# Attention block and quantised MLP on one core: seven of the eight rows of reciprocal deviations made by two transfers through DRAM

## The chip, the core and the metric

The kernel runs on one core of a Trainium2 chip. The metric is the time of one launch on the device in microseconds (us), as the median of the runs shown. The shortened names are those of the profile: PE is TensorE, PEld its weight loads, DVE VectorE, ACT ScalarE, POOL GpSimd, SP SyncE; SPq is SP's queue of DMA issues.

## The reference, cut to what matters

```python
def reference(x, ctx, g_xattn, g_ffn, Wq, ...):
    # x: (2, 2048, 512); ctx: (2, 77, 512); 16 heads of 32
    q = proj(_layernorm(x), Wq, bq)          # (x - mean) / sqrt(var + 1e-5), per token
    k, v = proj(ctx, Wk, bk), proj(ctx, Wv, bv)
    attn = softmax(q @ k.T / sqrt(32)) @ v   # per head
    x = x + tanh(g_xattn[0]) * (attn @ Wo.T + bo)
    h = gelu(_qlinear(_layernorm(x), w1, b1))  # inputs and weights rounded to 8 bits per tensor
    x = x + tanh(g_ffn[0]) * _qlinear(h, w2, b2)
    return x                                  # all in float32
```

The part that matters here is the first layer norm. Its mean is taken out by centring `Wq`; its factor 1/sqrt(var + eps) differs from token to token and is multiplied onto the projected q.

## The kernel before

The 4096 tokens are worked through in `NC` = 8 chunks of `CH` = 512 tokens, each of `TT` = 4 tiles of 128 tokens. The program has three stages, each a block of its own: `attention` (until some 337 us), `hidden` (first matmul of the MLP) and `output` (second). Only `attention` is touched. In it five instruction streams are written out by hand, one per engine, and meet at semaphores; their order is the order of the calls in each engine's `first_step`, `step(i)` for i = 1 to 7 (`LAST` = 7) and `last_steps`. `AHEAD` = 2: chunk 2's q is projected partly in step 1.

q is computed transposed, with features on the partitions and tokens along the row. So the factor of a token has to lie along the row too, the same on all 128 partitions: that is the tile `row` (128x512). It is made per chunk n like this:

- DVE's `stats1(n)` (L980, L984) gives mean and variance with the tokens on the partitions; POOL's `rstd_1(n)` (L1248, L1252) makes `rstd1`, 128x4: element (p, t) belongs to token 128 t + p.
- PE's `row_turn(n)` (L413) makes four 128x128 transposes of the broadcast columns of `rstd1` into a bank of PSUM.
- ACT's `row_copy(n)` (L760) copies that bank into `row`. It waits until q of the chunk before is scaled, as there is one `row`.
- DVE's `q_scale(n, m)` (L999), m = 0 to 3, multiplies each of the four banks of projected q by `row`.

From there the chain inside a step runs over three engines, once for each of four feature blocks m: PE's `project_q(i, m)` (L475), DVE's `q_scale(i, m)` (L999), ACT's `q_high(i, m)` (L780), PE's `scores_by_token(i, m)` (L488), DVE's `token_max(i, m)` (L1017), with DVE's `q_low(i, m)` (L1003) in between. `scores_by_token(i, m + 1)` writes the banks that `token_max(i, m)` reads, and waits for it. After the fourth, PE's `transpose_max(i)` (L502) turns the maxima. PE fills the time with pieces of the output projection of chunk i-2 (`project_out`, L578), in step 1 with chunk 2's projection (`project_q_ahead`, L453). `row_turn(i + 1)` stands in step i right behind `scores_by_token(i, 2)`, `row_copy(i + 1)` on ACT behind `q_high(i, 3)`:

```python
project_q(i, 3)
scores_by_token(i, 2)
if i < LAST:
    row_turn(i + 1)
if older:                      # i >= 2
    pe.wait_ge(q_lo_on, KD * i + 3)
    project_out(i - 2, 2, 0, 7)
...
scores_by_token(i, 3)
```

The last step, i = 7, has the same order but no next chunk, so no `row_turn`. `row_turn(1)` stands in PE's `first_step`, between the sums of head group 1 and `scores_by_key(0, 3)`; behind that comes `values(0, 2)` (L534), which waits for ACT's `c_copy(0, 1)` (L804). On ACT `c_copy(0, 1)` stands behind `xt_high(1, 2)` and `xt_high(1, 3)` (L774), which read the tile `xr` that SP loads.

SP issues nearly all transfers, in one order. Around the change that is, at the end of chunk 0: `load_x(2)`, `load_xt(1, 2)`, `load_xt(1, 3)` (L347, 256 KB of transposed x each into one of two slots of `xr`, once POOL's `xt_low` has freed it), four `load_xt_ahead` (L351, 256 KB each), `load_x(3)` (L340, 1 MB). Then per step: four `load_xt` of the next chunk, `load_x` of a later one, `store_x1` of an older one. ACT issues transfers only at the start.

Of the kernel before, what the change touches and what calls it, by code (L numbers as in the profile page):

```python
# [14 lines left out]
F32 = mybir.dt.float32  # L15
# [7 lines left out]
P = 128  # L23
# [39 lines left out]
def program(nc, x, x_t, ctx_t, wq_t, wk_t, wv_t, wo_t, bq, bk, bv, bo, w1_t, b1, w2_t, b2, g_xattn, g_ffn,  # L63
            eye, group_ones, out):
    with ExitStack() as whole:
# [21 lines left out]
        sh.ps = whole.enter_context(nc.psum_tensor("ps", [P, 8, 512], F32))  # L87
        sh.x1_dram = nc.dram_tensor("x1_dram", [NC, P, TT, D], F32, kind="Internal").ap()
# [38 lines left out]
def attention(nc, sem, sh, x, x_t, ctx_t, wq_t, wk_t, wv_t, wo_t, bq, bk, bv, bo, w1_t, b1, g_xattn, g_ffn,  # L127
# [8 lines left out]
    with ExitStack() as own:  # L136
# [103 lines left out]
        row_on = sem("row_on")  # L240
        q_scaled = sem("q_scaled")
# [66 lines left out]
        def rstd_value(c):  # L308

            return c + 1  # L310
# [15 lines left out]
        with nc.Block() as block:  # L326
            @block.sync
            def _(sp):
# [19 lines left out]

                def load_xt_ahead(k):
                    sp.wait_ge(w_lo_on, KD)  # L350
                    sp.dma_start(wo_raw[:, k, :], xt_v[k, AHEAD]).then_inc(xt_ahead_in[k], 16)  # L351
# [29 lines left out]
                load_x(2)  # L381
                load_xt(1, 2)
                load_xt(1, 3)
                for k in range(KD):
                    load_xt_ahead(k)
                sp.wait_ge(v_on, B)
                load_x(3)
                for i in range(1, NC):
                    n = i + 1
                    if AHEAD < n < NC:  # L390
                        load_xt(n, 0)
                        load_xt(n, 1)
                        load_xt(n, 2)
                        load_xt(n, 3)
                    if W1_T // TT <= i + 2 < NC:
                        load_x(i + 2)
                    if i >= 2:
                        store_x1(i - 2)
# [5 lines left out]
            def _(pe):  # L404
                def row_turn(n):

                    pe.wait_ge(ln1_rstd, rstd_value(n))
                    if n >= 2:
                        pe.wait_ge(c_on, GROUPS * (n - 1))
                    elif n == 1:  # L410
                        pe.wait_ge(v_on, B)
                    for t in range(TT):
                        mm = nc.tensor.transpose(ps[:, row_bank(n), t * P:(t + 1) * P],  # L413
                                                 rstd1[:, t:t + 1].to_broadcast([P, P]), sh.ident[:])
                    mm.then_inc(row_mm, 1)
# [43 lines left out]
                def project_q(c, m):  # L459
                    if m >= 2:  # L460
                        pe.wait_ge(q_lo_on, KD * c + m - 1)
                        if c == AHEAD:
                            pe.wait_ge(x1_on, TT * (c - 2) + m - 1)
                    elif c >= 2:
                        pe.wait_ge(x1_on, TT * (c - 2) + m + 1)
                    elif m == 0:
                        pe.wait_ge(v_on, 1)
                    else:
                        pe.wait_ge(row_on, 2)
# [23 lines left out]
                def transpose_max(c):  # L493
                    pe.wait_ge(smax_on, KD * c + KD)
                    if c == 0:
                        pe.wait_ge(q_lo_on, KD)
                    elif c < LAST:
                        pe.wait_ge(row_on, c + 2)
                    else:
                        pe.wait_ge(c_on, GROUPS * c)  # L500
# [102 lines left out]
                def first_step():  # L603
# [28 lines left out]
                    for g in range(1, GROUPS):  # L632
                        scores_by_key(0, g)
                        values(0, g - 1)
                        sums(0, g - 1)
                        if g == 2:
                            row_turn(1)

                def step(i):
# [15 lines left out]
                    if i < LAST:  # L655
                        row_turn(i + 1)
# [79 lines left out]
            def _(act):  # L736
# [100 lines left out]
                def first_step():  # L837
# [31 lines left out]
                    row_copy(1)  # L869
                    c_copy(0, 2)  # L870

                def step(i):
# [16 lines left out]
                    if nxt:  # L889
                        row_copy(n)  # L890
# [70 lines left out]
            def _(dve):  # L961
# [33 lines left out]
                def q_scale(c, m):  # L995
                    dve.wait_ge(q_mm, KD * c + m + 1)
                    dve.wait_ge(row_on, c + 1)
# [247 lines left out]
            def _(pool):  # L1245
                def rstd_1(c):
# [3 lines left out]
                    if c:  # L1250
                        pool.wait_ge(row_mm, c)
# [722 lines left out]
```

## Time and profile before

| | |
|---|---|
| median of 3 runs | 580.91 us (580.72 to 581.07) |
| the profiled execution | 581.38 us, of it 579.6 us span |
| PE busy | 565.7 us (98%), 3272 matmuls |
| DVE, ACT, POOL busy | 442.1 (76%), 336.6 (58%), 300.8 us (52%) |
| granted TensorE clock | 0.999 |
| DMA | 106.62 MB, mean 184 GB/s |

Busy matmuls are modelled with their ends overlapping the next one's start: in attention a 128x512 matmul is shown with some 0.39 us but follows its neighbour after 0.23 us, so a PE that is busy all the time can still have short waits inside. They are better read from the starts. In the timeline a row is one instruction, or a run of equal ones (x4), with start, duration, engine, line, operation, output and inputs, and in brackets the engine's idle time before it with what ended it.

### The profile page before, as it was taken

What the parts mean: (1) busy time and instruction counts of PE and PEld (TensorE: products, weight loads), DVE (VectorE), ACT (ScalarE), POOL (GpSimd) and SP (SyncE); (2) the same over time, 40 slices, a digit from 0 to 9 for tenths busy, and PEclk for the clock granted to TensorE, in tenths of its full rate; (3) what the DMA queues carried; (4) which work ended last, traced back from release to release, by engine and by line L of the source; (5) the groups of instructions that cost most, each with busy time, mean ns of one, the idle gap of its engine ahead of it and who ended that gap; (6) DMA issues with size and microseconds to landing.
All of it is one profiled execution on the core that took longest, in us unless ns stands there. A gap on an engine that the chain in (4) does not pass through costs nothing. (4 is left out here: it accounts for less than half of the span.)

```text
span 579.6 us, 9118 instructions
## 1 busy us (share of the span) xinstructions
PE 565.7 (98%) x3272; PEld 321.6 (55%) x3272; DVE 442.1 (76%) x622; ACT 336.6 (58%) x408; POOL 300.8 (52%) x242
## 2 busy tenths in 40 slices
PE   6999999999999999999999989999999999999997
PEld 3834746567476575674765854444444544444443
DVE  4698986979878698695895778788887799835282
ACT  3355374763855737438247538777786696555350
POOL 5457565762763666716072429655507247503383
PEclk9999999999999999999999999999999999999999
DMA  8966000411503305111001169987778995979766
GB/s 310 384 280 219 1 2 0 155 65 31 185 4 110 110 0 183 37 37 75 0 1 74 72 217 336 368 325 278 284 278 327 368 320 217 340 297 390 228 235 218
DMA packets 41944, 106.62 MB, mean 184 GB/s; under 512 B 3377, under 2 KB 4145, under 8 KB 37297
## 3 DMA queue, kind: packets, MB, share of 16 engines
q1 hardware_dynamic: 39952, 103.70, 48.8%
q10 hardware_dynamic: 1952, 2.42, 1.2%
q8 instruction: 23, 0.38, 0.3%
q14 instruction: 17, 0.13, 0.1%
HBM read 64.16 MB, written 41.94 MB: 183 GB/s over the span
## 5 line engine op out<-in xcount | busy, mean ns | idle before, releaser
L1552 PE MATMUL ps<-h_sb,w_q 128*128 (+1 forms) x488 | 109.7, 379 | 0.1
L1851 PE MATMUL ps<-w_q,h_q 128*128 128x512 bf16 x448 | 96.9, 379 | 0.0
L1934 POOL TENSOR_TENSOR xo<-xo,b2s 128x512 f32<-128x512 f32 x32 | 52.5, 1672 | 70.4 <-DMA xo<-x_dram 52.4
L1552 PEld LDWEIGHTS ps<-h_sb,w_q 128*128 128x128 bf16 x488 | 46.7, 98 | 52.2 <-issue 1.1
L1851 PEld LDWEIGHTS ps<-w_q,h_q 128*128 128x128 bf16 x448 | 43.8, 98 | 52.9
L1619 ACT ACTIVATE xo<-ps,b1s,sc 128x1024 f32<-128x1024 f32 x48 | 57.6, 1205 | 20.0 <-PE ps L1552 16.7
L794 ACT ACTIVATE prob<-ps 77x1024 f32<-77x1024 f32 x64 | 61.7, 1013 | 10.6 <-PE ps L521 10.6
L1705 DVE TENSOR_REDUCE hmax<-xo 128x1024 f32 (+1 forms) x48 | 58.3, 1217 | 12.1 <-ACT xo L1619 11.4
L1738 POOL TENSOR_SCALAR y<-x,mean,rs 128x512 f32<-128x512 f32 x24 | 50.2, 2098 | 29.6 <-DVE xq L1686 23.2
L780 ACT ACTIVATE q_hi<-ps,bq_sb 128x512 fp32r<-128x512 f32 x32 | 22.0, 688 | 63.8 <-DVE ps L999 63.6
L1286 POOL TENSOR_TENSOR c_lo<-c_sb,c_hi 128x512 fp32r<-128x512 f32 x28 | 38.4, 1391 | 34.6 <-ACT c_hi L822 34.6
L1911 DVE SCALAR_TENSOR_TENSOR xo<-ps,hs,xo 128x512 f32<-128x512 f32 x32 | 23.3, 746 | 40.3 <-POOL xo L1934 39.8
L1256 POOL TENSOR_TENSOR xt_lo<-xr,xt_hi 128x512 fp32r<-128x512 f32 x24 | 30.6, 1296 | 34.7 <-ACT xt_hi L774 34.5
L1017 DVE TENSOR_REDUCE neg_max<-ps 128x16 f32<-128x1232 f32 x32 | 45.9, 1433 | 3.3 <-PE ps L488 3.3
L578 PE MATMUL ps<-wo_hi,c_hi 128*128 128x512 f32 x112 | 47.3, 422 | 0.0
L578 PE MATMUL ps<-wo_hi,c_lo 128*128 128x512 f32 x112 | 44.9, 401 | 0.0
L578 PE MATMUL ps<-wo_lo,c_hi 128*128 128x512 f32 x112 | 44.2, 395 | 0.0
L1883 ACT ACTIVATE h_q<-h_sb 128x2048 bf16<-128x2048 f32 x16 | 29.7, 1902 | 20.9 <-DVE h_sb L1904 11.0
L475 PE MATMUL ps<-xt_hi,wq_hi 128*128 128x512 f32 x104 | 41.7, 401 | 0.0
L475 PE MATMUL ps<-xt_hi,wq_lo 128*128 128x512 f32 x104 | 40.9, 393 | 0.0
L475 PE MATMUL ps<-xt_lo,wq_hi 128*128 128x512 f32 x104 | 40.7, 391 | 0.0
L1301 POOL TENSOR_TENSOR x<-x,bo_gate 128x512 f32<-128x512 f32 x32 | 40.3, 1293 | 0.1
(194 smaller groups left out, 1110.5 us busy)
## 6 DMA issues: line engine op xcount, KB each, us to landing
h_dram<-xo SPq DMA_DIRECT2D x48, 512.0 KB, 2.9
h_sb<-h_dram SPq DMA_DIRECT2D x16, 1024.0 KB, 11.2
x_dram<-x SPq DMA_DIRECT2D x8, 1024.0 KB, 3.9
xo<-x_dram SPq DMA_DIRECT2D x8, 1024.0 KB, 5.0
x<-h_dram SPq DMA_DIRECT2D x8, 1024.0 KB, 7.8
x<-in_x SPq DMA_DIRECT2D x7, 1024.0 KB, 7.1
out<-xo SPq DMA_DIRECT2D x7, 1024.0 KB, 8.5
xr<-in_x_t SPq DMA_DIRECT2D x24, 256.0 KB, 3.7
```

Source lines behind the costliest of these rows:

```text
L475: mm = nc.tensor.matmul(ps[:, q_bank(c, m), :], w[:, k, m * P:(m + 1) * P], r[:, k, :], start=(j == 0), stop=(j == len(terms) - 1))
L578: mm = nc.tensor.matmul(ps[:, bank, :], a[:, k, t * P:(t + 1) * P], w[:, k, :], start=(j == 0), stop=(j == len(terms) - 1))
L794: nc.scalar.activation(prob[0:NK, p % SLOTS, :].rearrange("p (s n) -> p s n", s=2), ps[0:NK, 2 * (p % 2):2 * (p % 2) + 2, :], ACT.Exp).the ...
L1017: nc.vector.tensor_reduce(neg_max[:, :, :].rearrange("p t (r j) -> p t r j", j=DK)[:, :, :, m], ps[:, 0:TT, 0:4 * NK].rearrange("p t (h n) ...
L1286: nc.gpsimd.tensor_tensor(lo[:, g, :], c_sb[:, g, :], hi[:, g, :].bitcast(F32), ALU.subtract).then_inc(c_lo_on, 1)
L1301: nc.gpsimd.tensor_tensor(xa, xa, sh.bo_gate[:], ALU.add).then_inc(xg_on, 1)
L1552: mm = nc.tensor.matmul(ps[:, 2 * (m % 2) + s, :], w1_q[:, k, m * P:(m + 1) * P], xq_t[:, one(2 * j + s), k, :], start=(k == 0), stop=(k = ...
L1619: nc.scalar.activation(dst.rearrange("p (s n) -> p s n", s=2), ps[:, bank:bank + 2, :], ACT.Gelu, bias=b1s[:, m:m + 1], scale=sc[:, 4:5]). ...
L1705: nc.vector.tensor_reduce(dst, src, AX.X, ALU.max, apply_absolute_value=True).then_inc(hmax_on, 1)
L1738: nc.gpsimd.tensor_scalar(y[:, n % YS, :], x1[:, n, :], sh.mean2[:, n:n + 1], rs2[:, n:n + 1], ALU.subtract, ALU.mult).then_inc(y_on, 1)
L1851: mm = nc.tensor.matmul(ps[:, 4 * s + t, :], h_q[s][:, m, t * P:(t + 1) * P], w2_q[:, m, :], start=(m == 0), stop=(m == MF - 1))
L1934: nc.gpsimd.tensor_tensor(xo[:, s, t, :], xo[:, s, t, :], b2s[:], ALU.add).then_inc(xb_on, 1)
```

## The change

For chunks 1 to 7 PE's `row_turn` and ACT's `row_copy` go. Their place is taken by two transfers that SP issues: `store_row(n)` writes `rstd1` (128x4) to a row of 512 words in DRAM, so that element (p, t) lands at word 128 t + p, and `load_row(n)` reads that row back, broadcast to 128 partitions (256 KB), into `row`. `load_row(n)` waits for the store's end, for `q_scaled` of the chunk before (as `row_copy` did) and for the row load before. Chunk 0 keeps the old way.

```diff
+        sh.row_dram = nc.dram_tensor("row_dram", [NC, CH], F32, kind="Internal").ap()
...
+                def store_row(n):
+                    sp.wait_ge(ln1_rstd, rstd_value(n))
+                    sp.dma_start(sh.row_dram[n].rearrange("(t p) -> p t", p=P), rstd1[:],
+                                 allow_slow_non_contiguous=True).then_inc(row_out, 16)
+
+                def load_row(n):
+                    sp.wait_ge(row_out, 16 * n)
+                    sp.wait_ge(q_scaled, scaled_count(n - 1, KD - 1))
+                    if n >= 2:
+                        sp.wait_ge(row_in, 16 * (n - 1))
+                    sp.dma_start(row[:], as_row(sh.row_dram[n]).to_broadcast([P, CH])).then_inc(row_in, 16)
...
                 sp.wait_ge(k_biased, GROUPS)
                 load_x(2)
+                store_row(1)
                 load_xt(1, 2)
                 load_xt(1, 3)
+                load_row(1)
                 for k in range(KD):
                     load_xt_ahead(k)
...
                 for i in range(1, NC):
                     n = i + 1
+                    if n < NC:
+                        store_row(n)
                     if AHEAD < n < NC:
                         load_xt(n, 0)
                         load_xt(n, 1)
+                    if n < NC:
+                        load_row(n)
+                    if AHEAD < n < NC:
                         load_xt(n, 2)
                         load_xt(n, 3)
...
     # row_turn
                     pe.wait_ge(ln1_rstd, rstd_value(n))
-                    if n >= 2:
-                        pe.wait_ge(c_on, GROUPS * (n - 1))
-                    elif n == 1:
-                        pe.wait_ge(v_on, B)
...
     # project_q(1, 1)
-                        pe.wait_ge(row_on, 2)
+                        pe.wait_ge(v_on, B)
...
     # transpose_max
-                    elif c < LAST:
-                        pe.wait_ge(row_on, c + 2)
                     else:
                         pe.wait_ge(c_on, GROUPS * c)
...
     # PE, first_step and step
-                        if g == 2:
-                            row_turn(1)
...
-                    if i < LAST:
-                        row_turn(i + 1)
...
     # ACT, first_step and step
-                    row_copy(1)
...
-                        row_copy(n)
...
     # q_scale
-                    dve.wait_ge(row_on, c + 1)
+                    if c:
+                        dve.wait_ge(row_in, 16 * c)
+                    else:
+                        dve.wait_ge(row_on, 1)
...
     # rstd_1
-                    if c:
-                        pool.wait_ge(row_mm, c)
+                    if c == 1:
+                        pool.wait_ge(row_mm, 1)
+                    elif c:
+                        pool.wait_ge(row_out, 16 * (c - 1))
```

How this moves the instructions stands below at the two places that the prediction speaks of. On PE, in step 2 around the turn for chunk 3 (`k_hi,q_hi` are the scores by token, `wo` pieces of the output projection, `neg_max` the turned maxima), before:

```order
L488 MATMUL ps<-k_hi,q_hi 128x308 [waits smax_on,q_hi_on]
L488 MATMUL ps<-k_hi,q_hi 128x308 x3
L413 MATMUL ps<-ident,rstd 128x128 [waits c_on,ln1_rstd]
L413 MATMUL ps<-ident,rstd 128x128 x3
L578 MATMUL ps<-wo_hi,c_hi 128x512 [waits q_lo_on]
...
L578 MATMUL ps<-wo_hi,c_hi 128x512
L488 MATMUL ps<-k_hi,q_hi 128x308 [waits smax_on,q_hi_on]
L488 MATMUL ps<-k_hi,q_hi 128x308 x3
...
L502 MATMUL ps<-ident,neg_max 128x128 [waits row_on,smax_on]
```

and now:

```order
L506 MATMUL ps<-k_hi,q_hi 128x308 [waits smax_on,q_hi_on]
L506 MATMUL ps<-k_hi,q_hi 128x308 x3
L594 MATMUL ps<-wo_hi,c_hi 128x512 [waits q_lo_on]
...
L594 MATMUL ps<-wo_hi,c_hi 128x512
L506 MATMUL ps<-k_hi,q_hi 128x308 [waits smax_on,q_hi_on]
L506 MATMUL ps<-k_hi,q_hi 128x308 x3
...
L518 MATMUL ps<-ident,neg_max 128x128 [waits c_on,smax_on]
```

The four transposes are gone from between the two score groups, and `transpose_max` waits for `c_on` in place of `row_on`. The same goes for steps 3 to 6.

On SP, from the load of x of chunk 2 on, before:

```order
L340 DMA x<-in_x 128x4x512 [waits x_in,k_biased]
L347 DMA xr<-in_x_t 128x512 [waits xt_lo_on] x2
L351 DMA w_i<-in_x_t 128x512 [waits w_lo_on] x4
L340 DMA x<-in_x 128x4x512 [waits x_in,v_on]
L347 DMA xr<-in_x_t 128x512 [waits xt_lo_on] x4
L340 DMA x<-in_x 128x4x512 [waits w1_narrow,x_in]
L357 DMA x_dram<-x 128x2048 [waits x1_on]
```

and now, in which `row_dram<-rstd` is `store_row` and `row<-row_dram` is `load_row`:

```order
L343 DMA x<-in_x 128x4x512 [waits x_in,k_biased]
L354 DMA row_dram<-rstd 128x4x1 [waits ln1_rstd]
L350 DMA xr<-in_x_t 128x512 [waits xt_lo_on] x2
L362 DMA row<-row_dram 128x512 [waits q_scaled,row_out]
L366 DMA w_i<-in_x_t 128x512 [waits w_lo_on] x4
L343 DMA x<-in_x 128x4x512 [waits x_in,v_on]
L354 DMA row_dram<-rstd 128x4x1 [waits ln1_rstd]
L362 DMA row<-row_dram 128x512 [waits row_in,q_scaled,row_out]
L354 DMA row_dram<-rstd 128x4x1 [waits ln1_rstd]
L350 DMA xr<-in_x_t 128x512 [waits xt_lo_on] x2
L362 DMA row<-row_dram 128x512 [waits row_in,q_scaled,row_out]
L350 DMA xr<-in_x_t 128x512 [waits xt_lo_on] x2
```

The store of row 1 now stands ahead of `xr` for (1, 2) and (1, 3), and the load of row 1 between them and the four loads ahead. From chunk 3 on all loads of `xr` stand behind the store of their chunk's row, and the last two also behind the load of the row.

## Rows read from the trace of the kernel before

**Rows 1.** Busy times by stretch: PE, PEld, DVE, ACT, POOL; last clock, DMA share, GB/s.

```profile
60.00:100.00 40.00, 39.84 (x258) 25.29 (x257) 32.11 (x52) 22.27 (x31) 21.92 (x20) 1.00 0.00 1
100.00:300.00 200.00, 199.97 (x1293) 128.24 (x1295) 163.27 (x249) 112.08 (x162) 110.33 (x103) 1.00 0.21 72
```

**Rows 2.** The copy's instructions (L760) in the whole run, ns min/median/max.

```profile
L760 ACT COPY row<-ps x8: 578/579/587, 23.3 to 254.1; 128x512 f32<-128x512 f32 x8
```

**Rows 3.** Timeline of step 6, around the turn for chunk 7.

```profile
253.09 0.60 PE L413 MATMUL ps<-ident,rstd 128*128 128x128 f32 x4
253.34 1.43 DVE L1017 TENSOR_REDUCE neg_max<-ps 128x16 f32<-128x1232 f32 x1
...
253.45 0.48 PE L578 MATMUL ps<-wo_hi,c_hi 128*128 128x512 f32 x1
...
255.17 0.72 PE L488 MATMUL ps<-k_hi,q_hi 128*128 128x308 f32 x4
...
255.92 1.44 DVE L1017 TENSOR_REDUCE neg_max<-ps 128x16 f32<-128x1232 f32 x1 [0.50 <-PE ps L488]
...
257.42 0.20 PEld L502 LDWEIGHTS ps<-ident,neg_max 128*128 128x128 f32 x2 [0.34 <-DVE neg_max L1017]
```

**Rows 4.** Timeline of step 7, the same place without a turn.

```profile
291.64 1.43 DVE L1017 TENSOR_REDUCE neg_max<-ps 128x16 f32<-128x1232 f32 x1
...
293.19 0.58 PEld L488 LDWEIGHTS ps<-k_hi,q_hi 128*128 128x128 f32 x4 [0.44 <-issue]
...
294.07 1.44 DVE L1017 TENSOR_REDUCE neg_max<-ps 128x16 f32<-128x1232 f32 x1 [0.34 <-PE ps L488]
...
295.56 0.20 PEld L502 LDWEIGHTS ps<-ident,neg_max 128*128 128x128 f32 x2 [0.35 <-DVE neg_max L1017]
```

**Rows 5.** Timeline of DVE, step 1, to chunk 2's first scaling.

```profile
66.00 0.70 DVE L999 TENSOR_TENSOR ps<-ps,row 128x512 f32<-128x512 f32 x1 [0.63 <-PE ps L475]
66.61 1.43 DVE L1017 TENSOR_REDUCE neg_max<-ps 128x16 f32<-128x1232 f32 x1
...
69.02 1.44 DVE L1017 TENSOR_REDUCE neg_max<-ps 128x16 f32<-128x1232 f32 x1 [0.32 <-PE ps L488]
70.42 0.70 DVE L999 TENSOR_TENSOR ps<-ps,row 128x512 f32<-128x512 f32 x1
...
74.89 0.75 DVE L1003 SCALAR_TENSOR_TENSOR q_lo<-ps,bq_sb,q_hi 128x512 fp32r<-128x512 f32 x1 [0.74 <-ACT q_hi L780]
```

**Rows 6.** Timeline of DVE, step 2, third and fourth maxima.

```profile
100.30 1.43 DVE L1017 TENSOR_REDUCE neg_max<-ps 128x16 f32<-128x1232 f32 x1
...
102.74 1.44 DVE L1017 TENSOR_REDUCE neg_max<-ps 128x16 f32<-128x1232 f32 x1 [0.35 <-PE ps L488]
```

**Rows 7.** Timeline at the end of chunk 0, SP and POOL and ACT and PE.

```profile
40.38 1.26 POOL L1252 TENSOR_TENSOR rstd<-ve,minus_half 128x4 f32<-128x4 f32 x1
...
42.78 1.57 SPq L347 DMA_DIRECT2D xr<-in_x_t  x2
...
44.40 1.85 SPq L351 DMA_DIRECT2D w_i<-in_x_t  x4
...
46.89 0.65 PE L413 MATMUL ps<-ident,rstd 128*128 128x128 f32 x4
46.96 0.61 ACT L774 CAST xt_hi<-xr 128x512 fp32r<-128x512 f32 x1
...
48.37 0.62 ACT L774 CAST xt_hi<-xr 128x512 fp32r<-128x512 f32 x1 [0.80 <-DMA xr<-in_x_t]
...
49.62 1.06 PE L534 MATMUL ps<-prob,v 128*32 128x512 f32 x8 [0.99 <-ACT c_sb L804]
```

**Rows 8.** Landing of the 24 loads of xr (L347), us from issue.

```profile
DMA to landing us min/median/max: 2.8/3.7/11.3
```

**Rows 9.** DMA packets between 18.2 and 18.6 us.

```profile
DMA packets 205, 0.09 MB, mean 218 GB/s; under 512 B 132, under 2 KB 173, under 8 KB 205
```

**Rows 10.** DMA queue of SP between 41.5 and 48.5 us.

```profile
q1 hardware_dynamic: 621, 1.14, 57.7%
```

More of the change, by code:

```diff
@@ L240, in attention @@
         row_on = sem("row_on")
+        row_out = sem("row_out")
+        row_in = sem("row_in")
         q_scaled = sem("q_scaled")
```

## The prediction

> **What bounds the kernel now.** I read the busy times by stretch first: over 200 us of attention PE is busy for 199.97 us [rows 1]. Read by itself, this says that whatever leaves PE is won whole. But the ends of matmuls are modelled, and short waits hide in them, so the second look goes to the timeline at the place of the change. In step 6 the turn starts at 253.09 and the next matmul at 253.45, so it holds PE for 0.36 us; the fourth maximum on DVE (L1017) starts at 255.92, and `transpose_max` (L502) at 257.42, released by DVE [rows 3]. DVE's third maximum starts at 253.34. Step 7 has the same order without a turn, and so shows what is left when the turn goes: there PE's weight loads stand still for 0.44 us ahead of the fourth score (L488), the fourth maximum starts 294.07 - 291.64 = 2.43 us behind the third, and L502 again waits for DVE, for 0.35 us [rows 4]. With the turn the same distance is 255.92 - 253.34 = 2.58 us [rows 3]. So this place is bound by the chain score, maximum, score, maximum over PE and DVE, and the turn lies mostly in a wait that is there anyway. The rest of a step is PE's, so what this place gives reaches the end.
>
> **The change part by part.** Seven of the eight turns go, four matmuls each [rows 3], and seven of the eight copies of 579 ns on ACT [rows 2].
>
> *Steps 3 to 6 (turns for chunks 4 to 7).* From the third maximum to L502 it is 257.42 - 253.34 = 4.08 us with a turn [rows 3] and 295.56 - 291.64 = 3.92 us without [rows 4]. That is 0.16 us a step, 0.64 us for four. The bound above is the 0.36 us that PE is held, 1.44 us for the four; I take the lower since step 7 is the very same code. Nothing is lost on DVE or ACT, which only move with it.
>
> *Step 2 (chunk 3).* The two maxima are 102.74 - 100.30 = 2.44 us apart [rows 6], already step 7's 2.43 us, as DVE is late here: the turn was hidden. Gain 0, at most 0.36.
>
> *Step 1 (chunk 2).* 69.02 - 66.61 = 2.41 us [rows 5]: gain 0, at most 0.36. Here alone the new path is short of time. The load of row 2 has to wait for the last scaling of chunk 1, which starts at 66.00 and takes 0.70 [rows 5], and the first scaling of chunk 2 wants the row at 70.42 [rows 5]: 3.7 us. The load has the size and the shape of a load of `xr`, whose landing takes 2.8 us at the least and 3.7 in the median [rows 8]. So it comes just in time. What DVE can bear beyond that is at least the 0.74 us that it idles later ahead of `q_low(2, 0)` [rows 5]. Cost 0; its cover is that slack, and without it the wait passes into the divisions and on to the output projection of chunk 0. The other six rows are asked for as early and wanted only in the next step.
>
> *The copies on ACT.* In steps ACT waits behind them for L502 anyhow; `xt_high` comes 0.5 us sooner, and nobody waits for it. 0.
>
> *Waits moved.* POOL's next factors now wait for the store of the row before, a step old by then: 0. SP now waits for POOL's factors ahead of loads of `xr`; for chunk 3 two of them move from the end of chunk 0 behind step 1, for the others they move by the last `xt_low` and the factors, two or three instructions of POOL, at the end of a step. All are wanted by `xt_high` only after the fourth projection of the next step: 0. `project_q(1, 1)` and `transpose_max` wait for something earlier than before: 0.
>
> *The end of chunk 0 (turn for chunk 1).* PE's turn at 46.89 wins nothing by itself, as PE then waits 0.99 us for ACT's `c_copy(0, 1)` until 49.62, and ACT had waited 0.80 us, until 48.37, for the second load of `xr` [rows 7]. So here a transfer sets the time. Both loads are issued within 42.78 to 44.35, and the four loads ahead come right behind them from 44.40 [rows 7]: the late one needed some 4.3 us. The change alters its company. Behind it, SP now stops for the end of the store of row 1 and then issues the load of that row, so the four loads ahead come later. In front of it stands the store: POOL has the factors at some 41.4 (its instruction starts at 40.38 and the next at 41.36) [rows 7], and SP sends 512 separate words, since neighbouring words of a partition lie 128 apart in DRAM. How long these take is the one price that the trace does not have. Bound from below: at 18.2 to 18.6 us the queues moved 205 packets in 0.4 us, 132 of them under 512 B [rows 9]; at that pace 512 are through in 1.0 us, before the first load of `xr` gets going. Bound from above by packets of 2 KB: 57.7% of 16 engines for 7 us is 64.6 us for 621 packets, 104 ns each [rows 10], so 512 on 16 engines hold them for 3.3 us. With 1 us from an issue to its first packet (my estimate, inside the shortest landing of 2.8 us [rows 8]) the store begins at 42.4 and is done at 43.4 or at 45.7, and the first load of `xr`, issued at 42.78, would begin at 43.8 without it. In the first case the second load of `xr` lands in the median 3.7 us [rows 8] after some 44.0, at 47.7, and ACT wants it at 46.96 + 0.61 = 47.57 [rows 7]: the 0.80 us are won nearly whole. In the second it lands up to 1.9 us later than that, 1.2 us after the old 48.37: a loss. The value lies nearer to the small packets' pace, because these are small packets, but reads are not writes; I take half of the gain, 0.4 us.
>
> The Trainium skill has a rule against just this edit: "DMA: Bandwidth & Descriptors", section "Rules for kernel authors", says that a strided last dimension becomes one descriptor per element and should be rearranged; section "Specifications" adds that under 512 B an engine reads, changes and writes back. No row here shows such a write. By it the store would be the third rival below, not the sum.
>
> **Sum** against the profiled execution, 581.38 us: 0.64 + 0.4 = 1.0, so 580.4 us. It stands 0.47 above the median of the three runs; against that median, 580.91 - 1.0 = **579.9 us**. 0.2% is 1.16 us, about what a measurement of this kernel can tell from no change; the forecast lies just within it.
>
> **The rivals.**
>
> *The transfer gap closes whole, and more of the turns comes back.* 0.64 + 0.80 = 1.44 us: 579.5. For it: the late load loses its company of four, and the words may be through before it begins. Against it: the unknown write. With 0.3 from step 1 or 2 it is 579.2. Chance 0.31.
>
> *PE is bound as its 99.98% says.* Every turn returns its 0.36 us [rows 3]: 7 x 0.36 = 2.5 us, 578.4. For it: PE's busy time [rows 1]. Against it: step 7 [rows 4], and the wait of 0.99 us behind the first turn [rows 7]. Chance 0.09.
>
> *The store blocks the loads of `xr` (slower).* Each word costs the engines a read and a write of the price of a whole packet, 2 x 104 ns [rows 10]: 512 of them hold 16 engines 6.7 us, from 42.4 to 49.1. If the same queue serves its transfers in order, the first load of `xr` then starts 5.3 us later than 43.8, and the second lands near 53.0, 4.6 us after the old one. ACT and PE wait that long once: 4.6 - 0.64 = 4.0 us more, 584.9. It decides from about 120 ns a word, where the loss passes 1.8 us. The other six stores stand where `xr` is wanted only much later. The rule of the Trainium skill on transfers under 512 B (same page, "Specifications") is this case. Chance 0.09.
>
> *Row 2 lands late (slower).* If the load of row 2 takes as long as the longest of `xr`, 11.3 us [rows 8], it lands 7.6 us after it is wanted; less the slack of 0.74 this is up to 6.9 us, less 1.0 of gain: 586.8. It decides when landing passes some 6 us (3.7 to the need, 0.74 of slack, 1.8 to leave the 0.2%). Against it: between 60 and 100 us the DMA engines are idle (share 0.00) [rows 1], so nothing is in its way. Chance 0.04.
>
> That the change does not do what it says is no rival: in the order of the changed program the turns and copies are gone.
>
> **How the numbers follow.** Forecast 0.47, within 0.2%. Faster: 0.31 + 0.09 = 0.40. Slower: 0.09 + 0.04 = 0.13. The range leaves out most of the full return of the turns and most of the slow cases, and takes in a small loss at the first loads (up to 1.2 us at 104 ns a word, and some beyond): 578.8 to 582.0.
>
> **What would show it.** In steps 3 to 6 the third and fourth maximum should stand 2.43 us apart in place of 2.58, with a wait ahead of the fourth score like that of step 7. Steps 1 and 2 should keep 2.41 and 2.44. At the end of chunk 0 PE's wait ahead of L534 tells the rest: if what it waits for comes at 48.8, the whole gap was won; if after 49.6, the store was in the way. The first scaling of chunk 2 should start with a wait under 0.8 us. The forecast is wrong if the median lies under 579.2 (more of the turns was PE's than step 7 shows) or above 581 (a transfer is waited for).

## The result and the profile after

The changed kernel takes 592.0 us (median of 4 runs, 590.9 to 592.9) against 580.99 us of the kernel before beside it: a ratio of 1.0186, 95% interval 1.0171 to 1.0201, or 11.0 us more. 579.9 us were forecast, in a range of 578.8 to 582.0. The profiled execution took 592.02 us, 590.2 us of it span, where the one before had 579.6.

The page shows little of it: PE is busy for 566.7 us in place of 565.7. What differs are the small packets.

```profile
span 590.2 us, 9062 instructions
...
PE 566.7 (96%) x3244; PEld 319.2 (54%) x3244; DVE 441.9 (75%) x622; ACT 333.4 (56%) x401; POOL 300.9 (51%) x242
...
DMA packets 46647, 108.47 MB, mean 184 GB/s; under 512 B 7184, under 2 KB 7952, under 8 KB 42000
```

3377 packets under 512 B before, 7184 now: of the 3807 more, 7 x 512 = 3584 are the words of the seven stores.

**Where the time went: one mark per step.** The transposes of the maxima (L502 before, L518 now) come once a step, so their starts date the loss. Before they start at 36.82, 70.52, 104.23, 142.53, 180.82, 219.12, 257.42 and 295.56 us; now (six of the eight) at:

```profile
36.63 0.42 PEld L518 LDWEIGHTS ps<-ident,neg_max 128*128 128x128 f32 x4 [1.55 <-DVE neg_max L1030]
...
80.27 0.42 PEld L518 LDWEIGHTS ps<-ident,neg_max 128*128 128x128 f32 x4 [0.55 <-DVE neg_max L1030]
...
115.13 0.42 PEld L518 LDWEIGHTS ps<-ident,neg_max 128*128 128x128 f32 x4 [0.34 <-DVE neg_max L1030]
...
153.25 0.42 PEld L518 LDWEIGHTS ps<-ident,neg_max 128*128 128x128 f32 x4 [0.34 <-DVE neg_max L1030]
...
267.60 0.42 PEld L518 LDWEIGHTS ps<-ident,neg_max 128*128 128x128 f32 x4 [0.34 <-DVE neg_max L1030]
...
305.71 0.42 PEld L518 LDWEIGHTS ps<-ident,neg_max 128*128 128x128 f32 x4 [0.34 <-DVE neg_max L1030]
```

From mark to mark: from the first to the second 43.64 in place of 33.70 us (+9.94; the end of chunk 0 and step 1), then 34.86 in place of 33.71 (+1.15), four times 38.12 on average in place of 38.30 (-0.18 each), then 38.11 in place of 38.14. These add up to +10.3; -0.2 at the first mark and some +0.5 behind attention make up the 10.6 us by which the span grew. So almost all of the loss is one event early on, and the gain of steps 3 to 6 is there. From the last mark to the end all kernels of this document run the same code, and yet their profiled executions take between 283.7 and 285.6 us for it. Differences of 1 us between whole times are therefore better read from the marks.

**The event.** Timeline of the changed kernel, SP's DMA issues with the row:

```profile
41.49 0.38 SPq L354 DMA_DIRECT2D row_dram<-rstd  x1
42.60 1.58 SPq L350 DMA_DIRECT2D xr<-in_x_t  x2
50.84 0.33 SPq L362 DMA_DIRECT2D row<-row_dram  x1
69.36 0.38 SPq L354 DMA_DIRECT2D row_dram<-rstd  x1
77.39 0.34 SPq L362 DMA_DIRECT2D row<-row_dram  x1
```

The load of row 1 waits for its store and is issued 9.35 us behind it; that of row 2, with no other transfer in the way, 8.03 us behind its own. ACT, PE and DVE, in the same stretch:

```profile
54.82 1.26 ACT L786 CAST xt_hi<-xr 128x512 fp32r<-128x512 f32 x2 [7.94 <-DMA xr<-in_x_t]
...
56.71 1.94 PE L550 MATMUL ps<-prob,v 128*32 128x512 f32 x8 [8.62 <-ACT c_sb L816]
...
64.17 1.06 PE L550 MATMUL ps<-prob,v 128*32 128x512 f32 x8
...
82.71 0.70 DVE L1012 TENSOR_TENSOR ps<-ps,row 128x512 f32<-128x512 f32 x1 [2.50 <-DMA row<-row_dram]
```

ACT waits 7.94 us for the second pair of `xr`, where it waited 0.80 [rows 7], and PE stands behind ACT's copy until 56.71 in place of 49.62: 7.1 us. The same eight matmuls of PE that start there take 1.94 us in place of 1.06, and the next such group starts at 64.17 in place of 54.44 (9.7 us later). So 2.6 us more go between those two. The granted clock says why:

```profile
50.00:55.00 5.00, 0.00 (x0) 0.00 (x0) 2.99 (x3) 0.18 (x1) 0.00 (x0) 0.71 0.64 118
55.00:60.00 5.00, 3.29 (x16) 0.68 (x16) 0.00 (x0) 3.95 (x6) 4.48 (x4) 0.50 0.97 340
60.00:65.00 5.00, 5.00 (x24) 3.17 (x24) 0.70 (x1) 0.00 (x0) 5.00 (x5) 0.77 0.16 60
```

Columns as in [rows 1]: PE did nothing from 50 to 55 us, and from 55 to 60 us the clock granted is 0.50, which is 1.2 of 2.4 GHz; before, these windows show 1.00. The 0.71 from 50 to 55 us shows that the clock fell while PE was still waiting; the price of 2.6 us is paid after the wait. Last, row 2 comes 2.50 us late for chunk 2's first scaling.

**What the DMA engines did.** The same two stretches in the DMA view, of the changed kernel:

```profile
DMA packets 528, 0.00 MB, mean 2 GB/s; under 512 B 528, under 2 KB 528, under 8 KB 528
```

```profile
DMA packets 97, 0.19 MB, mean 28 GB/s; under 512 B 9, under 2 KB 9, under 8 KB 96
...
q1 hardware_dynamic: 96, 0.18, 58.8%
```

The first is 42.0 to 43.2 us: it holds 528 small records, the 512 words among them, and the view of 42.3 to 42.9 us still holds all 528. So all the words have their packet record within 0.6 us, and by its records the store is quick, quicker even than its lower bound of 1.0 us in the prediction. The second is 45 to 52 us: 97 packets in 7 us, with the engines counted as 58.8% busy. 0.588 x 16 x 7 us / 96 is 690 ns a packet; before, in the same 7 us, 1126 packets of SP's queue went through at 94.5%, 94 ns each. Part of the fall in number is that SP, which waits for the store, has issued less; the pace of a packet is the fairer measure, and the first experiment below has the same issues as before. The words leave the queue at once, and what stands behind them nearly stands still.

### The profile page after: what moved, and what is told of

The parts are those of the page before. It is cut to its first block and busy times, and to the rows that moved or that the text cites. A ratio compares the mean times of both kernels' runs of the same rounds, so it can differ in the third digit from the quotient of the medians.

```text
span 590.2 us, 9062 instructions
## 1 busy us (share of the span) xinstructions
PE 566.7 (96%) x3244; PEld 319.2 (54%) x3244; DVE 441.9 (75%) x622; ACT 333.4 (56%) x401; POOL 300.9 (51%) x242
## 2 busy tenths in 40 slices
DMA packets 46647, 108.47 MB, mean 184 GB/s; under 512 B 7184, under 2 KB 7952, under 8 KB 42000
## 5 line engine op out<-in xcount | busy, mean ns | idle before, releaser
L1720 DVE TENSOR_REDUCE hmax<-xo 128x1024 f32 (+1 forms) x48 | 58.2, 1217 | 12.9 <-ACT xo L1634 12.2
L550 PE MATMUL ps<-prob,v 128*32 128x512 f32 x256 | 34.8, 615 | 8.6 <-ACT c_sb L816 8.6
```

Source lines behind the costliest of these rows:

```text
L550: mm = nc.tensor.matmul(ps[DK * r:DK * (r + 1), BC, :], v[:, batch(c), h * DK:(h + 1) * DK], prob[:, (h // 2) % SLOTS, (h % 2) * CH:(h % 2 ...
L1720: nc.vector.tensor_reduce(dst, src, AX.X, ALU.max, apply_absolute_value=True).then_inc(hmax_on, 1)
```

## The experiments

Two theories at first. **W**: the 512 scattered words hold up every transfer behind them in SP's queue (the third rival of the prediction). **Q**: the loss comes from the new waits of SP and POOL and from rows that land late. All kernels are the changed one with one edit unless it says otherwise, and all have a kernel before run on the same chip beside them (581.4 to 582.2 us).

### One store alone, added to the kernel before

```diff
+                store_row(1)
                 load_xt(1, 2)
                 load_xt(1, 3)
```

All turns, copies and waits stay those of the kernel before; nobody reads what is stored.

> The kernel before, all turns kept, with one thing added: the store of row 1 (512 separate words to DRAM), issued ahead of the two loads of xr; nothing reads it. Theory W (the scattered words take some 9 us to land and hold up the loads issued behind them): ACT waits some 8 us for xr, PE some 8 us ahead of L534, the granted clock falls, 590 to 591 us. Theory Q (the loss comes from the new waits on SP and from rows that land late, not from the store as such): 581.0, PE's wait stays at 1 us.

Measured: 591.44 us, ratio 1.0177 [1.0156, 1.0199], 0.4 us above W's band. One transfer of 2 KB, whose result is not used, costs 10 us, nearly as much as the whole change. Its timeline:

```profile
41.50 0.38 SPq L353 DMA_DIRECT2D row_dram<-rstd  x1
...
55.33 1.27 ACT L782 CAST xt_hi<-xr 128x512 fp32r<-128x512 f32 x2 [8.43 <-DMA xr<-in_x_t]
...
57.23 1.94 PE L542 MATMUL ps<-prob,v 128*32 128x512 f32 x8 [8.79 <-ACT c_sb L812]
```

SP issues here all that it issued before, and in its queue 162 packets pass from 45 to 52 us in place of 1126, with the engines busy for 70.2%: 485 ns each. W holds for the event at the end of chunk 0, Q is out for it. The next period is 33.74 us, as before: step 2's loss is not from this store.

### The first store behind the loads of xr

```diff
-                store_row(1)
                 load_xt(1, 2)
                 load_xt(1, 3)
+                store_row(1)
                 load_row(1)
```

> The changed kernel with the store of row 1 issued behind the two loads of xr in place of ahead of them. Theory W: xr lands by 48 us, PE's wait of 8.6 us and the slow clock go; the row itself, with 8 to 9 us for the store and 3.2 for the load from 44.4 us on, lands at 56 to 57 and is late by 2 to 3 us for the first scaling of chunk 1; the late row 2 (+1.15) stays. In all 582 to 585 us. Theory Q: the order of the store against the loads does not matter, 591 to 592.

Measured: 586.04 us, ratio 1.0072 [1.0044, 1.01]; 1 us above W's band (the profiled execution took 585.22), and far below Q's. ACT's wait for `xr` at this place is gone and the clock is 1.00 throughout. What is left are the rows themselves:

```profile
45.21 0.43 SPq L354 DMA_DIRECT2D row_dram<-rstd  x1
53.00 0.33 SPq L362 DMA_DIRECT2D row<-row_dram  x1
...
58.16 0.70 DVE L1012 TENSOR_TENSOR ps<-ps,row 128x512 f32<-128x512 f32 x1 [4.15 <-DMA row<-row_dram]
...
65.71 0.79 PE L506 MATMUL ps<-k_hi,q_hi 128*128 128x308 f32 x4 [2.24 <-DVE neg_max L1030]
```

Its seven stores land 7.8 to 11.3 us after their issue. So moving the store saves 6 us, and 4.4 us stay against the kernel before on the same chip: row 1 comes 4.15 us late, where 2 to 3 were expected, and row 2 comes 2.61 us late.

### Transfers only from chunk 3 on

The turns of chunks 1 and 2 come back, with their copies and waits; chunks 3 to 7 go by transfers.

> Chunks 0 to 2 by the turn as before, chunks 3 to 7 by the two transfers. If the gain of 0.16 to 0.18 us a step in steps 3 to 6 is all that the removed turns are worth, and a store that nobody waits for costs nothing, 580.3 us (-0.7). If every removed turn is worth the 0.36 us that PE is held by it, 579.2. If the stores also slow something in the steps (loads of xr, stores of x), 581 or more.

Measured: 580.99 against 581.67 us, ratio 0.9992 [0.9982, 1.0002]. The difference of the medians is what was expected, but the interval holds 1. The marks from step 2 to step 6 stand 38.13, 38.11, 38.10 and 38.12 us apart, where the kernel before has 38.30, so the 0.18 us a step is real and shown by the profile; the median of the runs can't tell it from nothing. The five stores still land 10.0 to 12.2 us after issue, with loads of `xr` behind them, but from chunk 3 on these have time: ACT's longest wait for one is 1.31 us.

This run shows one thing more. The end of chunk 0 is the old code here, and yet ACT does not wait for `xr` there, and PE starts its group of values without a wait:

```profile
48.76 1.06 PE L554 MATMUL ps<-prob,v 128*32 128x512 f32 x8
```

In the trace of the kernel before it starts at 49.62 us, after ACT's wait of 0.80 [rows 7], and the first two marks stand 32.81 us apart here in place of 33.70. So that wait comes and goes between executions of the same code, and what a kernel wins or loses there below some 1 us can't be put down to its edit.

### TensorE kept at work in its wait

```diff
                         scores_by_key(0, g)
+                        if g == GROUPS - 1:
+                            pe.wait_ge(v_on, B)
+                            idle_turns(nc, sh, W1, 100)
                         values(0, g - 1)
```

`idle_turns` are transposes of the identity into a bank that nobody reads. The theory here is that 2.6 us of the loss are the clock's.

> The changed kernel with 100 transposes of the identity on PE ahead of values(0, 2), where it waits for ACT, so that PE has work during the wait. Theory: 2.6 us of the loss are PE running at the lower granted clock after its long wait (from 56.7 to 62.3 us); with PE kept at work the clock stays at 1.0 and the time is 589.4. Rival: the slow stretch costs nothing since the wait behind it is another engine's, 592.

Measured: 595.17 us, ratio 1.0249 [1.0221, 1.0277], slower than the changed kernel. In the profile the clock is 1.00 in every window from 45 to 65 us, and the two groups of values are 4.84 us apart, where the changed kernel has 7.46 and the kernel before 4.82:

```profile
47.75 11.14 PE L60 MATMUL ps<-ident 128*128 128x128 f32 x100
58.81 1.06 PE L550 MATMUL ps<-prob,v 128*32 128x512 f32 x8
...
63.65 1.06 PE L550 MATMUL ps<-prob,v 128*32 128x512 f32 x8
```

That is the clock's part, 2.6 us, shown at its place. But with 100 turns the values start 2.1 us later than in the changed kernel (58.81 in place of 56.71), and the time won did not stay: row 2 now comes 4.39 us late instead of 2.50 and the next period is 36.72 us in place of 34.86. The profiled execution took 592.84 us, 2.3 us less than the median, so the trace doesn't show the whole loss. It was run again with 72 turns, 8 us.

> The changed kernel with 72 idle transposes for TensorE in the place of its 8.6 us of waiting before the third values of chunk 0 (100 of them took 11.1 us, which was 2.1 us more than the wait). They take 8.0 us, so that they end before the wait does. Theory C (2.6 us of the 11 us lost are the lower clock that follows the wait): the granted clock stays 1.0 from 45 to 65 us, the last values of chunk 0 start at 61.5 us in place of 64.2, and the kernel takes 589 to 590 us. Rival (those 2.6 us would be lost anyway, since row 2 comes late for step 2): 591.5 to 592 us, with VectorE's wait for the row of chunk 2 longer than the 2.5 us of the changed kernel.

Measured: 596.86 us, ratio 1.0276 [1.0238, 1.0314]; both expectations were wrong. Here the first row's load came 10.2 us behind its store (9.35 in the changed kernel), ACT waited 9.62 us for `xr`, PE still waited 2.3 us after its idle turns, the clock fell all the same (0.86 from 55 to 60 us, 0.80 from 60 to 65), and row 2 was 4.44 us late, with its load issued 9.0 us behind its store. The next period is 38.30 us long, in place of 34.86, and in it the clock fell once more, to 0.68 from 92 to 94 us and 0.50 from 94 to 96, behind PE's waits of 2.02 and 0.86 us. As a mend this is worth nothing. In both kernels with idle turns the rows' loads come about a microsecond later behind their stores; whether the turns do that stays open, as landings spread from 7.8 to 12.2 us in the kernels without them.

### What makes the words slow: how many, or where they go

Three kernels, in which only the words of the store change. In the first, 128 of the 512 are stored, side by side:

```diff
-  sp.dma_start(sh.row_dram[n].rearrange("(t p) -> p t", p=P), rstd1[:],
+  sp.dma_start(sh.row_dram[n].rearrange("(t p) -> p t", p=P)[:, 0:1], rstd1[:, 0:1],
```

> The changed kernel, but each store writes 128 of the row's 512 words (128 packets of 4 bytes in place of 512), and the row is loaded from the input x in its place, so that the factors of chunks 1 to 7 are not the reference's; all the rest is as it was. In the changed kernel the store issued at 69 us, with no other transfer behind it, is followed by its row's load after 8.0 us, and the first store after 9.3 us. Theory N (the store's price goes by the number of its words, 16 to 18 ns each, and everything behind it on the engines waits): a quarter of it, 2 to 3.5 us with the part that any transfer pays; ScalarE's wait for the third chunk-wise load of xr falls from 7.9 us to 1 to 2.5 us, TensorE's granted clock stays at 1.0 from 50 to 65 us, and the kernel takes 580.5 to 583.5 us. Theory F (the price is that of one store into DRAM that is read back, whatever it holds): 8 us again and 592 us.

In the second, all 512 in runs of four:

```diff
-  sp.dma_start(sh.row_dram[n].rearrange("(t p) -> p t", p=P), rstd1[:],
+  sp.dma_start(sh.row_dram[n].rearrange("(p t) -> p t", p=P), rstd1[:],
```

> The changed kernel, but the store writes all 512 words in runs of four (128 pieces of 16 bytes), so that the tokens' factors stand in another order in the row. Theory N, in the form that each separate piece costs 16 to 18 ns: 2 to 3.5 us to the row's load behind the store at 69 us, and 580.5 to 583.5 us, as with 128 words. If instead the bytes or the source's 4-byte elements count, the wait is 8 us again and the time 592 us.

In the third, all 512 as single words, 64 bytes apart:

```diff
-        sh.row_dram = nc.dram_tensor("row_dram", [NC, CH], F32, kind="Internal").ap()
+        sh.row_dram = nc.dram_tensor("row_dram", [NC, CH, 16], F32, kind="Internal").ap()
...
-                    sp.dma_start(sh.row_dram[n].rearrange("(t p) -> p t", p=P), rstd1[:],
+                    sp.dma_start(sh.row_dram[n][:, 0].rearrange("(t p) -> p t", p=P), rstd1[:],
```

> The changed kernel, but each of the 512 words goes to a place of its own, 64 bytes from the next; the row is loaded from the input x in its place, so its values are not the factors. Theory N (number of words alone): 8 us to the row's load behind the store at 69 us, ScalarE waits 8 us for xr, 592 us. Theory L (words that share a line of memory wait for one another, since each is a write of part of the line): 2 to 4 us to the row's load, and 580.5 to 584 us.

Measured: 128 words side by side 590.25 us, ratio 1.0167 [1.0142, 1.0193], with the first load of a row 8.5 us behind its store; runs of 16 bytes 581.27 us, 1.0003 [0.9982, 1.0025]; 512 words 64 bytes apart 580.92 us, 0.9996 [0.9981, 1.0011]. Theory N, a price per word, falls: a quarter of the words is nearly as slow as all, and all of them are quick when they are spread. Theory F, a price of any store that is read back, falls with the runs of 16 bytes, which are read back too. The time from a store's issue to its landing, as the views of that line give it (min, median, max), for the words spread by 64 bytes and for the runs:

```profile
DMA to landing us min/median/max: 1.8/2.0/2.5
```

```profile
DMA to landing us min/median/max: 1.4/1.6/1.9
```

With the words spread, from 45 to 52 us 1045 packets of SP's queue go through in place of 96, behind just the same 528 small records from 42.0 to 43.2 us:

```profile
DMA packets 1046, 1.95 MB, mean 279 GB/s; under 512 B 99, under 2 KB 99, under 8 KB 1045
...
q1 hardware_dynamic: 1045, 1.94, 93.5%
```

So what costs is not the number of small packets but that they go side by side into the same piece of memory.

### How large that piece is

Two kernels with fewer neighbours: 16 words side by side, and 512 words 8 bytes apart.

> The changed kernel, but each store writes 16 words only (the first 16 tokens' factors, 64 bytes side by side), and the row is loaded from the input x in its place, so its values are not the factors. With 128 words side by side the first row's load came 8.5 us behind its store, with all 512 words 9.3 us, with 512 words 64 bytes apart and with runs of 16 bytes 2.8 us, which is as early as SP can issue it. Theory L64 (the writes that fall into the same 64 bytes go one behind another, about 0.5 us each, and sixteen fall into each; different pieces of 64 bytes go beside each other): 16 words take as long as 128 or 512, 8 us, and the kernel takes 589 to 592 us. Rival L512 (the writes into the same 512 bytes go one behind another, about 0.06 us each; 128 words fill 512 bytes): 1 us and what any transfer pays, so 2.8 us between the issues and 579.5 to 582 us.

> The changed kernel, but the 512 words stand 8 bytes apart, so that half as many share a piece of memory as in the changed kernel, whatever that piece's size (up to 2 KB); the row is loaded from the input x in its place, so its values are not the factors. Theory L (the writes into the same piece go one behind another): half the price, 4 to 5.5 us from the first store's issue to its row's load, ScalarE waits 3 to 4.5 us for xr, and the kernel takes 583.5 to 587.5 us. Rival (only words that touch each other hold one another up): 2.8 us and 579.5 to 582 us, as with words 64 bytes apart.

Measured: 16 words 581.35 us, 0.9993 [0.998, 1.0006], landing after 1.4 us; 8 bytes apart 581.39 us, 1.0007 [0.9991, 1.0023], landing after 4.3 us in the median. The second is half of the changed kernel's, as theory L has it for the landing, but the time is not: it lies in the rival's band and not in L's, as ACT's two waits for `xr` add up to 1.5 us, not 3 or more. The first rules out pieces of 64 bytes, since those 16 words fill one. Pieces of 512 and of 256 bytes were left, and 64 words side by side tell them apart.

> The changed kernel, but each store writes 64 words only, 256 bytes side by side; the row is loaded from the input x in its place, so its values are not the factors. Stores seen so far, from issue to landing: 16 words side by side 1.4 us, 128 words side by side over 7 us (the first row's load came 8.5 us behind its store), 512 words 8 bytes apart 4.3 us. Theory L512 (writes into the same 512 bytes go one behind another at some 0.06 us each): 64 words take half of what 128 take, 3.5 to 5 us, ScalarE's waits for xr at chunk 0's end add up to under 4 us, and the kernel takes 580 to 584 us. Rival L256 (the unit is 256 bytes, at 0.12 us a write; 16 words then take 2 us): 64 words take as long as 128, 7.5 to 9 us, ScalarE waits over 6 us for xr, and the kernel takes 588 to 592 us.

Measured: 589.02 us (median of 2 runs), ratio 1.0126 [1.0062, 1.019]. From its view of the store's line, and ACT's timeline:

```profile
DMA to landing us min/median/max: 6.9/7.7/8.5
```

```profile
53.48 1.29 ACT L786 CAST xt_hi<-xr 128x512 fp32r<-128x512 f32 x2 [5.60 <-DMA xr<-in_x_t]
```

256 bytes of single words, an eighth of the row, already take nearly as long to land as all of it: 7.7 us, where the load of row 2 in the changed kernel came 8.0 behind its store. (The kernel as a whole loses less, 6.8 us, partly since no row is late for chunk 2: its next period is 33.70 us.) 5.60 us of ACT's wait lie just under the 6 us that the rival gave, but far above L512's. So the piece is 256 bytes or smaller, and larger than 64. In the Trainium skill, "DMA: Bandwidth & Descriptors", section "How a descriptor splits into AXI transactions" says that a transfer's pieces are moved in transactions of at most 256 bytes, each of which starts at a multiple of 256. The runs allow that size, but none shows that this is the cause.

In words that share 256 bytes and the median landing: 4 (64 bytes apart) 2.0 us, 16 (runs of 16 bytes) 1.6, 16 (16 words alone) 1.4, 32 (8 bytes apart) 4.3, 64 (64 words alone) 7.7. From 32 to 64 that is 3.4 us / 32 = 0.106 us a write. At 16 the same line would give 2.6 us, and less was measured, so a single price per write is too simple below 32; this stays open. Pieces of 128 bytes would fit worse: 16 words would then share one both at 8 bytes apart (4.3 us) and in the store of 16 words (1.4 us), unless the number of pieces counts as well, which no run varies by itself.

### The layout mended

Runs of 16 bytes are quick, but put the tokens in another order. One more edit puts it right, on the reader's side:

```diff
-                    nc.vector.tensor_tensor(bank, bank, row[:], ALU.mult).then_inc(q_scaled, 1)
+                    factor = row[:]
+                    if c:
+                        bank = bank.rearrange("a (t p) -> a t p", p=P)
+                        factor = row[:].rearrange("a (p t) -> a t p", p=P)
+                    nc.vector.tensor_tensor(bank, bank, factor, ALU.mult).then_inc(q_scaled, 1)
```

> The changed kernel with one edit that keeps what it computes: the store writes each partition's four factors side by side (128 pieces of 16 bytes in place of 512 of 4), and VectorE's scaling of q reads the row in a strided view that puts the tokens in order again. If the layout of the 4-byte writes is the whole loss, this is what the change was forecast to be: steps 3 to 6 0.18 us shorter each, no stall at chunk 0's end, 579.5 to 581 us against 580.9 to 581.7 of the kernel before on this chip, ratio 0.9975 to 1.000. Rival (the strided read slows VectorE, whose first scaling is in the chain of a step): 0.70 us scalings become 1 us or more and the kernel takes 581 to 584 us.

Measured: 586.86 us, ratio 1.0087 [1.0073, 1.0101]. The rival's mechanism was right, and its time, 581 to 584 us, was still too low. The view of the scaling's line:

```profile
L1016 DVE TENSOR_TENSOR ps<-ps,row x32: 690/1059/1202, 24.9 to 296.2; 128x512 f32<-128x512 f32 x32
```

Chunk 0 still reads `row` in order and takes 0.69 us; the strided read takes 1.06 in the median. (The edit also makes all three views of the instruction three-dimensional; no run separates that from the stride.) Steps 3 to 6 are 38.99 us long in place of 38.13 with the same store and an ordinary read: 0.86 us a step for four scalings that are 0.37 longer each, 1.5 us in all, of which more than half is on the path. Against the kernel before these four steps are 0.69 us longer each and step 7 0.81 us, 3.6 of the 5.4 us that this kernel loses. Putting the row in order on ACT instead wasn't tried. So no version is shown to be faster than the kernel before: the one from chunk 3 on comes nearest, with 0.7 us that the runs can't tell from nothing.

## Why the prediction was wrong

**What held.** The turns of steps 3 to 6 were forecast at 0.16 us each from step 7 [rows 3, 4]; measured 0.18. The third and fourth maxima of step 6 now stand as step 7's:

```profile
263.69 1.43 DVE L1030 TENSOR_REDUCE neg_max<-ps 128x16 f32<-128x1232 f32 x1
...
265.24 0.57 PEld L506 LDWEIGHTS ps<-k_hi,q_hi 128*128 128x128 f32 x4 [0.44 <-issue]
...
266.10 1.44 DVE L1030 TENSOR_REDUCE neg_max<-ps 128x16 f32<-128x1232 f32 x1 [0.32 <-PE ps L506]
```

2.41 us apart (2.43 forecast, 2.58 before), with the wait of 0.44 us ahead of the fourth score. That PE's 99.98% of busy time would not return 0.36 us a turn was right: the rival at 578.4 is out. Copies on ACT and POOL's wait cost nothing that the trace shows.

**The step that failed: the price of the store** in "The end of chunk 0". It was bounded by 1.0 us (pace of the small packets of another time [rows 9]) and 3.3 us (packets of 2 KB [rows 10]) and put near the lower end, "because these are small packets". Row 1's load came 9.35 us behind its store and row 2's 8.03. The records of the 512 packets lie within 0.6 us and so even undercut the lower bound; what it missed is that a packet's record is not the end of its write. Both bounds were paces at which packets pass an engine, and neither row showed a write into memory that a neighbour is writing too. Nothing in the trace had that pattern, and then the nearest rows bound nothing from above. The term (0.4 us of gain) should have been a loss of 9.7 us: 7.1 of waiting and 2.6 at the lower clock. The gain itself was read from a wait of 0.80 us in one trace, and another execution of the same code does not have that wait, so no run shows the 0.4 us either.

**The rival was named and priced too low.** "The store blocks the loads of `xr`" is the mechanism, with its place, ACT's wait for `xr`. It had 2 x 104 ns a word, 6.7 us on 16 engines where the row's load in fact followed after 9.35, 584.9 us and a chance of 0.09. Beyond the words it lacked two things: the lower clock behind PE's long wait, 2.6 us, and row 2. The rule of the Trainium skill against single elements ("DMA: Bandwidth & Descriptors", section "Rules for kernel authors") pointed the right way and deserved the larger chance. The other one, on transfers under 512 B (same page, "Specifications"), does not explain it by itself: 512 such packets, spread by 64 bytes, land in 2.0 us, and their kernel takes no longer than the one before.

**Row 2 in step 1** was to be just in time, from 3.7 us between the last scaling of chunk 1 and its need. The margin was counted from that scaling alone, as if the store had long landed. The scaling ends at 75.75 + 0.70 = 76.45 us, but the load is issued at 77.39, 0.94 us later, 8.03 us behind its store; it then takes until 82.71, 5.3 us, where its median is 3.2. It is 2.50 us late, and the next period 1.15 us longer. With the quick layouts (64 bytes apart, runs of 16) DVE does not wait for this row at all, so the step's own reckoning holds once the store is quick. The rival "row 2 lands late" happened as an outcome of the other.

**The check on the whole.** The kernel with words 64 bytes apart has all the parts of the change but the crowded writes (its row is read from the input x, so the values are others). It takes 580.92 against 581.38 us, 0.5 us less where 1.0 was forecast, with an interval from 1.1 us less to 0.6 more (0.9981 to 1.0011). That agrees with the sum and with no gain at all. Its profile shows the gain of steps 3 to 6 once more (38.12 us each in place of 38.30); of the rest of the sum, the 0.4 us at the end of chunk 0, the profiles can show nothing: with quick stores (64 bytes apart, runs of 16 bytes, 16 words) PE's group of values starts there at 48.75, 50.17 and 50.72 us, on both sides of the 49.62 before.

## What to carry to other kernels

Before a small tile is written to DRAM element by element, look where neighbouring elements go: single words side by side, from many partitions, took 7 to 12 us to land, as few as 64 of them 6.9 to 8.5 us, and all 512 took about 2 us when they stood 64 bytes apart or in runs of 16 bytes. And such a store isn't cheap by being small or unread: here the loads issued after it on the same queue waited with it. Putting it behind the loads that somebody waits for saved 6 of 11 us, and the reader of the row still waited. Where a rival's mechanism comes with no row at all that shows its pattern, its price is unknown above, and its chance should not shrink because the nearest rows are fast.

## What the hardware showed beyond that

- The packet records of 512 words all lie within 0.6 us, while the load that waits for the store is issued 8.0 and 9.4 us behind it. The cost shows in the packets behind them: 96 in 7 us, at 690 ns each, and with the store alone added 162 at 485 ns, in place of 1126 at 94 ns.
- With PE's wait of 8.6 us, until 56.71, the granted clock was 0.71 from 50 to 55 us, 0.50 from 55 to 60 and back at 1.00 from 65. In the kernel with the store moved behind the loads PE's waits there are 2.24 us and shorter, and the clock of the profiled execution stays at 1.00; in the one with 72 idle turns it fell behind a wait of 2.31 us and again behind one of 2.02. In the one with 100 turns a wait of 1.98 us left it at 1.00.
- A 128x512 multiplication on DVE that reads one operand from SBUF at a stride of four words took 1.06 us in place of 0.69, in three-dimensional views.
